# Key-stack one-hot copies as listed steps, row maxima over 64 rows, and a new list of steps, in a fused cross-attention, self-attention and mixture-of-experts kernel

## The reference

```python
# cross-attention, one head of width 128, over 512 context rows
q = layernorm(x) @ Wq + bq;  k = ctx @ Wk + bk;  v = ctx @ Wv + bv
x = x + tanh(g0) * softmax(q @ k.T / sqrt(128)) @ v
# block: self-attention with 16 heads of width 8, then a mixture of experts
X = layernorm(x);  h = rmsnorm(X, norm1_w)
attn = softmax(einsum('bshd,bthd->bhst', h @ wq, h @ wk) / sqrt(8))
X = X + (attn @ (h @ wv)) @ wo
h2 = rmsnorm(X, norm2_w)
combine = top-2 of softmax(h2 @ router_w), renormalised by a softmax, one-hot over 8 experts
out = X + swiglu(h2, shared) + sum_e combine[:, e] * swiglu_e(h2)      # width 128 -> 256 -> 128
x = x + tanh(g1) * out
```

## Time and profile before

| what | value |
|---|---|
| median of 3 runs | 221.26 us (218.88 to 221.61) |
| the profiled execution | 220.48 us, of which the span is 218.6 us |
| PE, PEld busy | 193.9 us (89%), 167.1 us (76%) |
| DVE, ACT, POOL busy | 139.4 us (64%), 106.8 us (49%), 54.6 us (25%) |
| DMA | 11.55 MB in 8998 packets |

### The profile page before, as it was taken

The page is one execution under the profiler, slowest core; times in us unless marked ns, Lnnn a source line. Parts: engine busy times, 40 slices in busy tenths (PEclk is TensorE's granted clock), DMA queues, the critical chain, the costliest instruction groups (busy, mean ns, idle before and its releaser), DMA issues.

```text
span 218.6 us, 4395 instructions
## 1 busy us (share of the span) xinstructions
PE 193.9 (89%) x1575; PEld 167.1 (76%) x1575; DVE 139.4 (64%) x357; ACT 106.8 (49%) x215; POOL 54.6 (25%) x88
## 2 busy tenths in 40 slices
PE   7388995997888979879898989988999999999994
PEld 5265764874866757657686859978999999999993
DVE  2604667789596766857774765889665564554653
ACT  2636374665477757958788734324222223223220
POOL 2917396122010075216841034300000000000000
PEclk9959999999999999999999999999999999999999
DMA  5941993055457935793200000000000000000000
GB/s 139 234 128 22 160 163 42 17 69 69 69 70 94 139 108 70 86 132 103 78 0 0 3 0 0 3 0 1 17 10 3 0 25 3 0 3 24 0 4 24
DMA packets 8998, 11.55 MB, mean 53 GB/s; under 512 B 976, under 2 KB 6992, under 8 KB 8752
## 3 DMA queue, kind: packets, MB, share of 16 engines
q1 hardware_dynamic: 8976, 11.27, 29.1%
HBM read 5.50 MB, written 0.52 MB: 28 GB/s over the span
## 4 chain that ended last, share of the span: by engine, by line
PE 76%; DVE 14%; ACT 4%; issue 3%; POOL 1%; DVEq 0%; POOLq 0%; ACTq 0%
PE bank L1117 14%; PE bank L1106 7%; PE bank L1105 7%; PE bank L1107 7%; PE bank L1088 7%; PE bank L1062 6%; PE bank L1073 5%; DVE mxs L849 4%; PE bank L939 4%; PE bank L954 3%; PE bank L1126 2%; PE bank L930 2%; ACT k_st L519 2%; PE bank L1010 1%; PE bank L946 1%
## 5 line engine op out<-in xcount | busy, mean ns | idle before, releaser
L849 DVE TENSOR_REDUCE mxs<-bank 128x2 f32<-128x512 f32 x64 | 41.4, 687 | 15.2 <-PE bank L1062 14.8
L637 ACT ACTIVATE ep<-bank 128x512 f32<-128x512 f32 x64 | 36.5, 605 | 14.1 <-PE bank L1073 13.6
L1105 PE MATMUL bank<-split,whi 128*128 128x256 f32 x144 | 43.2, 300 | 0.0
L1106 PE MATMUL bank<-split,whi 128*128 128x256 f32 x144 | 40.7, 283 | 0.0
L1107 PE MATMUL bank<-split,wlo 128*128 128x256 f32 x144 | 40.2, 279 | 0.0
L1117 PE MATMUL bank<-down_s,early 128*128 128x128 f32 x288 | 38.3, 276 | 2.1 <-DVE early L866 2.0
L657 ACT ACTIVATE early<-bank 128x512 f32<-128x512 f32 x28 | 16.7, 598 | 46.9 <-PE bank L1107 46.9
L1117 PEld LDWEIGHTS bank<-down_s,early 128*128 128x128 f32 x288 | 35.0, 191 | 2.6 <-DVE early L866 2.2
L869 DVE TENSOR_TENSOR early<-early,bank 128x512 f32<-128x512 f32 x28 | 19.3, 688 | 25.4 <-PE bank L1107 25.3
L1062 PE MATMUL bank<-k_st,q_st 80*128 80x256 f32 x128 | 29.7, 317 | 0.9 <-DVE mxs L849 0.5
L1105 PEld LDWEIGHTS bank<-split,whi 128*128 128x128 f32 x144 | 27.3, 190 | 0.0
(11 more groups left out here) (141 smaller groups left out, 274.2 us busy)
## 6 DMA issues: line engine op xcount, KB each, us to landing
raw<-expert_w SPq DMA_DIRECT2D x9, 256.0 KB, 8.2
k_st<-k_st SPq DMA_DIRECT2D x7, 256.0 KB, 5.8
q_st<-split SPq DMA_DIRECT2D x24, 64.0 KB
k_st<-split SPq DMA_DIRECT2D x24, 64.0 KB
down_s<-expert_w SPq DMA_DIRECT2D x9, 128.0 KB, 8.0
early<-ctx_T SPq DMA_DIRECT2D x1, 672.0 KB, 9.3
xs<-x_tiles SPq DMA_DIRECT2D x2, 256.0 KB, 4.8
out_dram<-x SPq DMA_DIRECT2D x4, 128.0 KB, 1.8
```

The source lines that it names most:

```text
L637: nc.scalar.activation(ep[:, n % NEP].rearrange("p t s -> p (t s)"), b_of(("exp", n))[:], ACT.Exp, scale=SCALE_H).then_inc(free(("exp", n) ...
L849: nc.vector.tensor_reduce(mxs[:, half % 2, :, 64 + h:65 + h], b_of(("max", n))[:].rearrange("p (t s) -> p t s", t=TB), AX_X, ALU.max).then ...
L1105: pe.matmul(bank, whi[:, fs], h2hi[:, hs], start=True, stop=False)
L1106: pe.matmul(bank, whi[:, fs], h2lo[:, hs], start=False, stop=False)
```

## The change

- `copy_picks` is no longer at the head of ACT's program. Its two halves are steps `r0` and `r1` of `FIRST_STEPS`.
- The row-maximum matmuls read rows 0 to 63 of the stacks and not 0 to 79. So they no longer need the one-hot rows or cleared maxima, and the waits on `picks_ready` and `pads_ready` at slot 0 and slot 48 go; the wait on the picks moves to the first transposed scores. In the built program these 128 matmuls carry an array tile of 64 x 128; they carried 128 x 128, as their neighbours L1073 still do.
- The clears of the maxima rows (POOL, L410 and step `c3`, L429) go, and the two DMAs that spread the first of them (L324).
- All three tables of steps have new numbers; 12 items start inside the slots and take tanh, where 8 did.

```diff
-    0: [("mT0", 9, 9), ("mT1", 17, 17), ("uT0", 30, 31), ("uT1", 31, 31), ("cT", 32, 32),
+    0: [("mT0", 9, 11), ("mT1", 18, 18), ("uT0", 30, 31), ("uT1", 31, 31), ("cT", 31, 31),
...
-FIRST_STEPS = """f0 g0 xn0 f1 t0 f2 q0 s0 g1 s1 p0 xn1 z0 g2 xn2 p1 q1 o0 o1 s2 s3 f3 q2 p2 j0 p3 n0 s4 o2 h0 o3
-                 p4 k0 n1 g3 e0 xn3""".split()
+FIRST_STEPS = """f0 f1 g0 xn0 q0 g1 t0 s0 s1 f2 xn1 j0 g2 p0 r0 q1 p1 f3 o0 r1 s2 xn2 o1 z0 s3 q2 g3 n0 h0 p2 p3
+                 s4 o2 o3 k0 xn3 p4 n1 e0 h1 s5""".split()
...
-    NSEL = 64 + NH
+    NROW = 64
+    NSEL = NROW + NH
...
-            words, maxima = k_st[:].bitcast(F32), q_st[:].bitcast(F32)
+            words = k_st[:].bitcast(F32)
...
-            sp.dma_start(maxima[64:NSEL, s], maxima[64:NSEL, 0]).then_inc(padded[s], 16)
...
-            sp.wait_ge(pads_ready, 1)
...
-                nc.gpsimd.memset(q_st[64:NSEL, s].bitcast(F32), 0.0).then_inc(pads_ready, 1)
-                pool.wait_ge(pads_ready, s + 1)
...
-            def clear_maxima(b):
-                is_full(pool, ("exp", NH * (b - NSTACK + 1) - 1))
-                pool.wait_ge(w_split, 5)
-                nc.gpsimd.memset(q_st[64:NSEL, b % NSTACK].bitcast(F32), 0.0).then_inc(pads_ready, 1)
...
-            def copy_picks(s):
-
-                picks = ident[64:NSEL, 64:64 + NH].rearrange("r (g p) -> r p g", p=2)
-                for p in range(2):
-                    nc.scalar.copy(k_st[64:NSEL, s, p * NG:(p + 1) * NG, :],
-                                   picks[:, p].unsqueeze(2).broadcast_to([NH, NG, L])).then_inc(picks_ready, 1)
+            def copy_picks(p):
+
+                picks = ident[64:64 + NH, 64:64 + NH].rearrange("r (g p) -> r p g", p=2)
+                nc.scalar.copy(k_st[64:64 + NH, 0, p * NG:(p + 1) * NG, :],
+                               picks[:, p].unsqueeze(2).broadcast_to([NH, NG, L])).then_inc(picks_ready, 1)
 
             act.wait_ge(ident_ready, 1)
-            copy_picks(0)
...
-                    if b == 0 and half == 0:
-                        for i in range(1, NSTACK):
-                            act.wait_ge(padded[i], 64)
...
+                elif stage == "r":
+                    copy_picks(i)
...
-                    if n == 0:
-                        pe.wait_ge(picks_ready, 2)
                     if h == 0:
                         if 1 <= b < NSTACK:
-                            pe.wait_ge(padded[b], 64)
-                        else:
-                            pe.wait_ge(pads_ready, b // NSTACK + 1)
+                            pe.wait_ge(padded[b], 48)
...
-                                         q_st[0:NSEL, b % NSTACK, h // 2, j * P:(j + 1) * P],
-                                         k_st[0:NSEL, b % NSTACK, k_slot(h), :], start=True, stop=True)
+                                         q_st[0:NROW, b % NSTACK, h // 2, j * P:(j + 1) * P],
+                                         k_st[0:NROW, b % NSTACK, k_slot(h), :], start=True, stop=True)
...
+                    if n == 0:
+                        pe.wait_ge(picks_ready, 2)
```

More of the change, by code:

```diff
@@ L33 @@
 SEQ_STEPS = {
[5 rows of a table removed]
-        ("route_weights", 50, 58)],
[5 rows of a table removed]
-        ("route_weights", 90, 90)],
-}
-FIRST_STEPS = """f0 g0 xn0 f1 t0 f2 q0 s0 g1 s1 p0 xn1 z0 g2 xn2 p1 q1 o0 o1 s2 s3 f3 q2 p2 j0 p3 n0 s4 o2 h0 o3
-                 p4 k0 n1 g3 e0 xn3""".split()
[L49 to L52, removed]
[5 rows of a table added]
+        ("route_weights", 48, 55)],
[5 rows of a table added]
+        ("route_weights", 98, 99)],
+}
+FIRST_STEPS = """f0 f1 g0 xn0 q0 g1 t0 s0 s1 f2 xn1 j0 g2 p0 r0 q1 p1 f3 o0 r1 s2 xn2 o1 z0 s3 q2 g3 n0 h0 p2 p3
+                 s4 o2 o3 k0 xn3 p4 n1 e0 h1 s5""".split()
+MIXED_STEPS = {2: "m0 k1 p5", 3: "e1 q3", 4: "e2", 6: "o4 e3 o5 s6", 7: "s7 p6 n2 m1", 8: "h2", 10: "k2",
[3 rows of a table added]
 BANKS = {"turn": (0, 1, 6), "proj": (2, 3, 7), "sum": (4, 5), "misc": (4, 5)}
@@ L252, in flamingo_block @@
         zeros_ready, lower_ready = sem("zeros_ready"), sem("lower_ready")
-        pads_ready, picks_ready, sel_ready, k_half = sem("pads_ready"), sem("picks_ready"), sem("sel_ready"), sem("k_half")
+        picks_ready, sel_ready, k_half = sem("picks_ready"), sem("sel_ready"), sem("k_half")
         padded = [sem(f"padded{s}") for s in range(NSTACK)]
@@ L424, in select_rows @@
                         nc.gpsimd.tensor_copy(rows_k[:, :, :, part], one).then_inc(sel_ready, 1)
-            def clear_maxima(b):
-                is_full(pool, ("exp", NH * (b - NSTACK + 1) - 1))
-                pool.wait_ge(w_split, 5)
-                nc.gpsimd.memset(q_st[64:NSEL, b % NSTACK].bitcast(F32), 0.0).then_inc(pads_ready, 1)
-                pool.wait_ge(pads_ready, b - NSTACK + 2)
             def add_bias(b):
@@ L492, in _ @@
                     split_weights(i)
-                elif stage == "c":
-                    clear_maxima(i)
                 elif stage == "a":
```

## The result

The changed kernel takes 278.66 us (median of 4 runs, 276.55 to 280.60) against 220.44 (218.88 to 221.61) for the one before: ratio 1.2645, 95% interval 1.2513 to 1.2777. The prediction was 215.0 with a range of 212 to 226. The kernel loses 26% where a gain of 2.8% was forecast, and ends 63.7 us above the forecast.

The account below looks back on a forecast made before the run. PE bounds: its 65 us dense stretch cannot shorten, only begin sooner. From 220.48 us: -5.7 (slot 0) -0.5 (work done) -1.4 +0.6 -0.5 +0.3 +1 +0.7 (stack waits) = -5.5, so 215.0 us, range 212 to 226.

Parts of the forecast that it names:

- rival A: Slots: 61 stretches of 64-row tiles cost 0.23 us each, net 6 to 14, giving 224 us; chance 0.25.
- thinner stretch from 11 to 21 us: Start: named as a place where PE's clock might fall and make the forecast wrong; no size given.
- Part 1: Start: with the picks' casts off ACT's head, slot 0 comes at 31.0 us instead of 36.74, 5.7 us gained.
- so I keep the clock: Start: PE's pause shrinks from 4.1 us to about 0.7, so the clock stays at 2.4 GHz, worth 2.3 us.
- Part 2: POOL and pads before slot 0: clear ends at 23.5 us, pads issued at 26.5, 3.1 us later than before.
- Part 3: Stack DMAs behind the pads: batch 1's lands at 53.8 to 54.8 us; slots 16 and 48 wait briefly.
- terms of 0.7 and 1 us for the stacks: Added waits for stack data: 0.7 us at slot 16, 1 us at slot 48 (bounds 0 and 3.5).
- Rival B: Pads and stacks cap the gain: stack 1 lands at 57 us, slot 16 waits 3 us, 218.0 us; chance 0.13.
- Part 4: Slots: 64 rows gain nothing; moved steps give and cost small amounts, and four more tanh items add 0.3 us.
- credits of 1.4 and 0.5 and the 0.6 against them: Slots: later `mT0` of batches 2 and 3 gains 0.7 each, moved last pv group 0.5; `cT` loses 0.6.
- tanh term of 0.3: Dense stage: four more tanh items add four DVE passes, costing PE 0 to 1 us, taken as 0.3.
- Rival C: Start gives nothing: casts only move on ACT, PE waits 3.7 us and for the clock again, 220 us; chance 0.06.

Follow-up runs that it names:

- e2: The kernel before with only the row-maximum matmuls reading 64 rows instead of 80: 280.55 us.
- e3: e2 with the transposed score matmuls over 64 rows too, so the maximum is not subtracted: 233.56 us.
- e9: e1 with 22 fillers (matmuls over zeroed weights, results unread) in PE's waits before slot 9: 218.96 us, ratio 0.9935.
- e14: The kernel before, no 64-row tiles, with six 8-column matmuls ahead of each pair of maxima: 332.93 us, ratio 1.494.
- e12: e9 with POOL waiting, ahead of its first two splits of expert weights, for the same batch's second norm: 216.66 us, ratio 0.9798.
- e4: The kernel before with only the two casts of the picks made steps r0 and r1: 221.56 us, ratio 1.0011.
- e5: e4 with 17 fillers (matmuls over zeroed weights, results unread) in five waits of PE: 217.32 us, ratio 0.9816.
- e1: The changed kernel with maxima over 80 rows again and the clears, pad copies and waits these need: 221.51 us, ratio 1.0078.
- e11: The changed kernel, maxima over 64 rows, with the fillers of e9 in PE's waits of the start: 275.02 us, ratio 1.2477.

## Why the prediction was wrong, point by point

**Where it failed: rival A's price.** The forecast rests on "64 rows in place of 80 gain nothing", from the step of 0.12 at 80 and 128 rows. Both of those rows stood in one tile among their like, and the rows couldn't show what a change of the row tile costs. I had the rival, with the right mechanism (e2, e3) and a price of 0.23 us a stretch. Measured is 0.38 at full clock: I had taken the pv group as the pattern (0.09 in, 0.14 out), but each of the two changes costs 0.09 on the step over it and 0.10 on the next. I also took zero for the forecast because the 64-column tile "is the nearer in size", against the pv rows and against what the Trainium skill ("TensorEngine Tiling (Array Packing)", Key Properties) says of a changed tiling mode; that choice was wrong.

**What was missing altogether: the clock.** An estimate from the rows for the changed kernel: 102.4 us at half clock hold slots of 1.45 us that are 0.87 at full clock, so 61 us of work; with the other 13.6 us of half clock that leaves a span near 230. The same order over 80 rows has a span of 215.6 at a clock of 1.00 (e9). So the changes' own price is some 14 us, the 23 us of 61 stretches less what PE's idle time takes: the upper end of the 6 to 14 that I gave rival A. (e3, at nearly the old clock, lost 6 to 7 us by 94 changes.) The other 47 us of the changed kernel's 277.3 are the clock, and no term of the sum and no rival had them. I used PEclk only for the idle start. I read "busy" as "at its clock", and wrote down the "thinner stretch from 11 to 21 us" as the one danger for the clock. The stretch that lost it was the slots, and e14 shows that no tile need change for that; what exactly brings the clock down in the changed kernel stays open as said above.

**Part 1** was right by its rows and wrong in what it is worth. q0 at 7.87 (said 8.2), scores of tile 1 done at 11.13 (11.2), no five in slice 2. Slot 0 came at 32.93, not 31.0: most of the 1.9 us is the meeting of DVE and POOL, in the chain above as 2.13 us for two operations of 0.34; e12, without it, is at slot 0 1.7 us ahead of e9. The term "so I keep the clock" failed: it was kept there and lost at 33.2 to 40.0. The busy tenths of the kernel before have a five in slice 6, the waits ahead of slot 0, which the prediction didn't weigh. A lead of 2.9 us was gone within 8 us in e4, and came back whole with fillers (e5).

**Part 2**: clear done at 23.0 (said 23.5), pads issued from 26.3 (26.5). Right; but I moved the selection step and the clear on POOL and didn't ask what runs beside what once its queue is shorter. That is the 2.3 us by which e12 is ahead of e9.

**Part 3**: can't be read in the changed kernel, since its slots are slow. In e12, slot 16 stands at 54.02 (said 54.1 to 54.8) and slot 48 at 93.12 (said 91.5 asked, 92.5 with the wait). PE waits ahead of neither: slot 16 follows slot 15 after the plain 0.48 us. So the terms of 0.7 and 1 us for the stacks came to nothing in e12. Rival B, which had slot 16 at 57, falls.

**Part 4**: with 80 rows in both, slots 16 to 60 take 48.7 us in the old order (e5) and 50.2 in the new (e12), and what follows slot 60 takes 0.5 more. So the credits of 1.4 and 0.5 and the 0.6 against them didn't come to a gain of 1.3 but to a loss of 2.0. PE's waits in e12 show a part of it: a new one of 1.1 us for `mT1` (L1084 <- ACT q_st L603), and 2.3 for `cn` where e5 has 1.9. The dense part is the same (95.3 us in both from its first matmul to the end): the tanh term of 0.3 is nothing.

**Sum and rivals.** Without its 64 rows, with 22 fillers and with POOL's split out of the way, the change gives 215.13 in e12's profiled execution (median 216.66). That this is the number of the forecast is luck: the order lost 2.0 us behind slot 16 where 1.3 were to be gained, the stacks cost nothing where 1.7 stood in the sum, and the clock is kept by matmuls that the change doesn't have. Rival C (the start gives nothing) is what e1 and e4 show, mainly by the clock (in e1 by DVE and POOL too); it had named the clock beside PE's waits for the casts, but at an earlier place. Two slips of the working had no weight: slice 28 begins at 153 us and not at 148, and Part 3 moves slot 16 by the full 6.8 us of which the sum counts 6.2.

## What to carry to other kernels

Count how often neighbouring matmuls change the number of row groups they use (here 64 rows and more than 64): in this kernel 64 rows in place of 80 saved nothing, and each change cost 0.19 us. Read the granted clock beside the busy share in every stage, the fullest too: here it was at half for 102 us in a stage that read 96 to 98% busy. The microseconds won in the thin start were only won once PE's waits behind it were filled as well. And after any move ask which two engines now run side by side.

## What the runs showed of the hardware that I had not expected

- A change between a tile of 64 x 128 and one of 128 rows: 0.09 us on the step over it and 0.10 on the next one, at 2.4 GHz. Between 128 x 128 and 128 x 64 the step is a plain 0.12.
- PE 96 to 99% busy in the profile at 1.2 GHz for 102 us (changed kernel, e2, e11) and 136.5 us (e14), and back at 2.4 GHz in the dense part.
- A matmul of 8 columns with 128 columns of weights: 0.112 us at full clock (e14), nearly the 0.118 of one with 256 columns.
- DVE's 0.34 us operation takes 1.45 us beside a POOL operation of 1.28 us (e9).
- Nearly equal work and waits of PE (5.07 of 7.9 us and 4.91 of 7.7 busy), 2.9 us apart in time, and the clock falls behind them in one kernel and not in the other (e4 and before).
